# A gated cross-attention and quantised feed-forward kernel: first loads by halves, the last probabilities turned through a third bank, own result buffers for the last two tiles

## What is computed

```python
# attention, for each of 8 contexts; input1 = layernorm(x), input2 = ctx, both 256 x 512
theta_x = einsum('ld,bdt->btl', theta_w, input2) + theta_b        # latent 128
phi_x   = einsum('ld,bdt->blt', phi_w, input1) + phi_b
p       = softmax(einsum('btl,bls->bts', theta_x, phi_x))         # 512 x 512
g_x     = einsum('ld,bdt->btl', g_w, input1) + g_b
t_x     = einsum('bts,bsl->blt', p, g_x)
h       = relu((t_x - mean) * rsqrt(var + 1e-5) * ln_gamma + ln_beta)   # over 128 x 512
x       = x + tanh(g_xattn) * (einsum('ol,blt->bot', out_w, h) + out_b + input2)
# feed-forward; bitlinear(x, w) = quant8(rmsnorm(x)) @ ternary(w).T
x       = x + tanh(g_ffn) * bitlinear(silu(bitlinear(y, w1)) * bitlinear(y, w2), w3)   # y = layernorm(x)
```

## Time and profile before

| | |
|---|---|
| time, median of 3 runs | 303.57 us (303.13 to 303.72) |
| the profiled execution: its time | 304.05 us |
| its span, first to last instruction | 302.3 us |
| mean granted clock of TensorE | 0.999 of full speed |
| busy: TensorE, VectorE, ScalarE, GpSimd | 294.6, 240.7, 196.9, 194.1 us |
| attention, to the last context's last scores | about 119 us |
| passage | about 119 to 146 us |
| feed-forward, tiles 2 to 15 | about 146 to 302 us |

### The profile page before, as it was taken

How to read it: one execution, slowest core, us unless ns; L and a number is a source line. 1 busy time by engine, 2 the same in 40 slices (tenths; PEclk the granted TensorE clock), 3 DMA queues, 4 the chain that set the end, 5 groups by cost and what they waited for, 6 DMA issues and landing times.

```text
span 302.3 us, 4409 instructions
## 1 busy us (share of the span) xinstructions
PE 294.6 (97%) x1336; PEld 159.8 (53%) x1352; DVE 240.7 (80%) x541; ACT 196.9 (65%) x346; POOL 194.1 (64%) x294
## 2 busy tenths in 40 slices
PE   7899999999999999999999999999999999999995
PEld 5665757575757575544444444444444444444443
DVE  3799979796969796699988788887986896867862
ACT  1399898989989858787954736455455456355620
POOL 3360959594949187295988768576786786655710
PEclk9999999999999999999999999999999999999999
DMA  7999960496020001020325356144324351561354
GB/s 260 411 422 415 400 249 3 143 302 245 7 70 0 0 3 35 0 19 19 69 44 78 88 120 116 39 111 105 72 74 101 73 124 49 118 128 34 86 110 156
DMA packets 52792, 37.00 MB, mean 122 GB/s; under 512 B 43040, under 2 KB 43424, under 8 KB 51744
## 3 DMA queue, kind: packets, MB, share of 16 engines
q1 hardware_dynamic: 52480, 36.45, 42.4%
q10 hardware_dynamic: 288, 0.27, 0.3%
HBM read 22.02 MB, written 4.19 MB: 87 GB/s over the span
## 4 chain that ended last, share of the span: by engine, by line
PE 83%; DVE 6%; DMA 3%; issue 3%; SPq 2%; ACT 1%; POOLq 0%; DVEq 0%; POOL 0%
PE bank L1115 34%; PE bank L1133 14%; PE bank L1059 8%; PE bank L1039 7%; PE bank L1052 4%; PE bank L1074 4%; PE bank L1026 4%; PE bank L1018 3%; PE bank L1007 3%; DMA x<-x_dram 2%; DMA out_dram<-stage 1%; DVE stage L788 1%; SPq L266 1%; DVE x L726 0%; DVE xst L654 0%
## 5 line engine op out<-in xcount | busy, mean ns | idle before, releaser
L1115 PE MATMUL bank<-wq,stage 128*128 128x512 bf16 x499 | 112.4, 379 | 1.1 <-DVE x L726 0.4
L1115 PEld LDWEIGHTS bank<-wq,stage 128*128 128x128 bf16 x512 | 50.0, 98 | 62.4 <-issue 2.5
L788 DVE SCALAR_TENSOR_TENSOR stage<-bank,s,stage 128x512 f32<-128x512 f32 x64 | 47.5, 744 | 24.1 <-PE bank L1115 18.3
L543 ACT ACTIVATE xn<-stage 128x1024 f32<-128x1024 f32 x31 | 32.8, 1057 | 44.8 <-DVE stage L788 44.8
L535 ACT ACTIVATE stage<-bank,s 128x512 f32<-128x512 f32 x64 | 43.2, 681 | 17.0 <-PE bank L1115 14.8
L1133 PE MATMUL bank<-wq,prob 128*128 128x512 bf16 x221 | 50.3, 379 | 0.2
L409 POOL TENSOR_SCALAR stage<-stage,hsc 128x1024 f32<-128x1024 f32 x30 | 33.7, 1134 | 21.1 <-DVE hsc L819 21.1
L329 POOL TENSOR_SCALAR prob<-prob,rsum 128x512 f32<-128x512 f32 x30 | 20.2, 695 | 34.3 <-DVE rsum L690 34.3
L793 DVE TENSOR_REDUCE m<-stage 128x1 f32<-128x1024 f32 x31 | 37.7, 1215 | 0.8
L1039 PE MATMUL bank<-ph,th 128*128 128x512 f32 x96 | 36.0, 487 | 0.5 <-DVE ph L679 0.5
L1133 PEld LDWEIGHTS bank<-wq,prob 128*128 128x128 bf16 x224 | 21.9, 98 | 26.4
(11 more groups left out here) (113 smaller groups left out, 430.9 us busy)
## 6 DMA issues: line engine op xcount, KB each, us to landing
stage<-w1t_dram SPq DMA_DIRECT2D x4, 1024.0 KB, 12.0
stage<-w2t_dram SPq DMA_DIRECT2D x4, 1024.0 KB, 13.9
stage<-w3t_dram SPq DMA_DIRECT2D x4, 1024.0 KB, 6.5
out_dram<-stage SPq DMA_DIRECT2D x15, 256.0 KB, 2.3
x<-x_dram SPq DMA_DIRECT2D x7, 512.0 KB, 10.9
c_sb<-ctx_in_dram SPq DMA_DIRECT2D x7, 512.0 KB, 6.5
pc<-pack_c_dram SPq DMA_DIRECT2D x1, 640.0 KB, 16.0
x<-x_dram SPq DMA_DIRECT2D x2, 256.0 KB, 3.0
```

Source lines behind the costliest of these rows:

```text
L543: A.activation(junk, h_sb[t % 2][:, half * HF:(half + 1) * HF], ACT.Square, accum_out=ssq[:, half:half + 1]).then_inc(sq_done, 1)
L788: V.scalar_tensor_tensor(h_sb[k][:, c * 512:(c + 1) * 512], up_banks(n)[1][:, :], s12[:, u % 2, 1, k:k + 1], sil[n % 3], ALU.mult, ALU.mul ...
L1115: last = mm(bank[:, :], turned[:, row:row + P], wq[:, at:at + 512], start=q == 0, stop=q == KI - 1)
```

## The change

Loads: the halves of x 0 and context 0 go in turn, and `pack_b` goes as two DMAs, with a semaphore of its own for `g`'s weight. Eight warm-up matmuls stand where nine did. For context 0, GpSimd normalises three quarters and ScalarE the fourth, and `gated_context(0)` waits for `x_norm(0)`.

```diff
+        def result(t):
+
+            return c_sb[:, 1, t - (NT - 2)] if t >= NT - 2 else xo[t % 2]
...
+        def b_turn(i, c):
+
+            return banks[2] if (i, c) == (B - 1, 2) else banks[4] if i == B - 1 and c == 3 else b_pt[c % 2]
+
+        def turned_p(i, c):
+
+            return c_sb[:, 0, 0] if (i, c) == (B - 1, 2) else probT[:, 0] if i == B - 1 and c == 3 else probT[:, c % 2]
...
+        def b_total(k):
+
+            return banks[6] if k == 0 else b_st
...
             if n < 8:
-                return (pair0, pair0, pair2, pair0, pair2, pair1, pair0, pair2)[n]
-            return (pair0, pair2, pair1)[(n - 8) % 3]
...
+                return (pair0, pair2, pair0, pair2, pair0, pair1, pair2, pair0)[n]
+            return (pair2, pair0, pair1)[(n - 8) % 3]
...
             sp.dma_start(x2[:, 0:T], x_v[0][:, 0]).then_inc(xa_loaded, 16)
+            sp.dma_start(c_sb[:, 0, 0], c_v[0][:, 0]).then_inc(ca_loaded, 16)
             sp.dma_start(x2[:, T:2 * T], x_v[0][:, 1]).then_inc(x_loaded[0], 16)
-            sp.dma_start(c_sb[:, 0, 0], c_v[0][:, 0]).then_inc(ca_loaded, 16)
             sp.dma_start(c_sb[:, 0, 1], c_v[0][:, 1]).then_inc(c_loaded[0], 16)
-            sp.dma_start(pb[:, :], pack_b).then_inc(pb_loaded, 16)
+            sp.dma_start(pb[:, 0:D], pack_b[:, 0:D]).then_inc(pb_loaded, 16)
+            sp.dma_start(pb[:, D:2 * D], pack_b[:, D:2 * D]).then_inc(gw_loaded, 16)
...
+                if i == 0:
+                    pool.wait_ge(xn_ready, DH)
...
-                normalise(i - 1)
+                normalise(i - 1, TC - 1 if i == 1 else TC)
...
-                if 2 <= i <= 5:
+                if 3 <= i <= 5:
                     rounds((i - 2) // 2, 4 * (i % 2), 4 * (i % 2) + 2)
                 if i >= 2:
                     tx_root(i - 2)
-                if 2 <= i <= 5:
+                if i == 2:
+                    rounds(0, 0, 4)
+                elif 3 <= i <= 5:
                     rounds((i - 2) // 2, 4 * (i % 2) + 2, 4 * (i % 2) + 4)
...
             normalise(B - 1, 2)
+            rounds(2, 2, 3)
             tx_root(B - 2)
-            rounds(2, 2, 4)
+            rounds(2, 3, 4)
             prep_quant(1)
-            rounds(2, 4, 8)
+            rounds(2, 4, 6)
+            tx_root(B - 1)
+            rounds(2, 6, 8)
             root_h(0)
-            tx_root(B - 1)
             quant_h(0)
...
-                1: (None, (M, 0, 3), None, (M, 0, 4), None, (M, 0, 5), (M, 0, 6)),
-                2: ((M, 0, 7), (M, 1, 0), (M, 1, 1), (M, 1, 2), None, (M, 1, 3), (M, 1, 4)),
...
+                1: (None, None, None, (M, 0, 3), None, (M, 0, 4), (M, 0, 5)),
+                2: ((M, 0, 6), (M, 0, 7), None, (M, 1, 0), (M, 1, 1), (M, 1, 2), (M, 1, 3)),
...
                 act.wait_ge(pT_done, 4 * i + c + 1)
-                A.copy(probT[:, c % 2], b_pt[c % 2][:, :]).then_inc(pT_ready, 1)
+                A.copy(turned_p(i, c), b_turn(i, c)[:, :]).then_inc(pT_ready, 1)
...
+            def normalise(i):
+
+                act.wait_ge(rsum_ready, i + 1)
+                for c in range(2 if i else 3, TC):
+                    at = prob[:, i % 2, c]
+                    A.activation(at, at, ACT.Copy, scale=rsum[:, c:c + 1]).then_inc(pnorm_ready, 1)
...
-            act.wait_ge(rsum_ready, B)
-            for c in (2, 3):
-                A.activation(prob[:, 1, c], prob[:, 1, c], ACT.Copy, scale=rsum[:, c:c + 1]).then_inc(pnorm_ready, 1)
-            p_copy(B - 1, 0)
-            p_copy(B - 1, 1)
+            normalise(B - 1)
+            for c in range(TC):
+                p_copy(B - 1, c)
             silu(0, 0)
-            p_copy(B - 1, 2)
-            p_copy(B - 1, 3)
+            relu(B - 2)
             weight_sign(2, 0)
-            relu(B - 2)
+            silu(0, 1)
             weight_sign(2, 1)
-            silu(0, 1)
+            silu(0, 2)
             weight_sign(2, 2)
-            silu(0, 2)
...
             def down(t):
                 dve.wait_ge(dn_done, t + 1)
-                if t >= 2:
+                if 2 <= t < NT - 2:
                     dve.wait_ge(xo_free[t % 2], 16 * (t // 2))
-                V.scalar_tensor_tensor(xo[t % 2], b_down(t)[:, :], dq[:, t % 4:t % 4 + 1], x_tile(t), ALU.mult, ALU.add)\
+                V.scalar_tensor_tensor(result(t), b_down(t)[:, :], dq[:, t % 4:t % 4 + 1], x_tile(t), ALU.mult, ALU.add)\
                     .then_inc(xo_ready, 1)
...
+                if i == 0:
+                    low_part(i, ph, b_ph, 1, ph_ready, phl_ready)
                 if i + 1 < B:
                     x_stats(i + 1, 1)
                 else:
                     prep_scale(0)
-                if i == 2:
-                    weight_scale(0)
                 if i >= 3:
                     tx_dev(i - 2)
-                low_part(i, ph, b_ph, 1, ph_ready, phl_ready)
+                if i >= 1:
+                    low_part(i, ph, b_ph, 1, ph_ready, phl_ready)
                 if i == 2:
                     tx_dev(0)
...
+                if i == 2:
+                    weight_part(0)
+                row_max(i, 0)
                 if i == 0:
                     x_norm(1)
-                row_max(i, 0)
                 if i >= 2:
                     tx_var(i - 2)
                 if i >= 1:
                     residual(i)
                 row_max(i, 1)
+                if i == 2:
+                    weight_scale(0)
...
             tx_dev(B - 2)
             tx_gamma(B - 2)
             add_out(B - 3, 1)
-            hmul(0, 0)
             tx_var(B - 2)
             prep_max(1, 0)
             prep_max(1, 1)
             tx_norm(B - 2)
             prep_scale(1)
+            hmul(0, 0)
+            tx_mean(B - 1)
             row_stats(2, 0)
             row_stats(2, 1)
             prep_mean(2)
             hmul(0, 1)
-            tx_mean(B - 1)
+            add_out(B - 2, 0)
+            tx_dev(B - 1)
             hmul(0, 2)
-            absmax(0, 0)
-            add_out(B - 2, 0)
-            hmul(0, 3)
-            tx_dev(B - 1)
             add_out(B - 2, 1)
...
-            dve.wait_ge(xo_free[1], 16 * (NU - 1))
...
             def g(i):
-                if i >= 1:
+                if i == 0:
+                    pe.wait_ge(gw_loaded, 16)
+                else:
                     pe.wait_ge(exp_done, 4 * i)
...
-                if 4 * i + c >= 2:
-                    pe.wait_ge(pT_ready, 4 * i + c - 1)
+                if (i, c) == (B - 1, 2):
+                    pe.wait_ge(exp_done, 4 * B)
+                elif 4 * i + c >= 2:
+                    pe.wait_ge(pT_ready, 4 * i + c - 1 if (i, c) != (B - 1, 3) else 4 * i + 1)
                 if c == 1 and i >= 2:
                     pe.wait_ge(x2_ready, 2 * (i - 2) + 1)
                 for tc in range(TC):
-                    last = tr(b_pt[c % 2][:, tc * P:(tc + 1) * P], prob[:, i % 2, tc, c * P:(c + 1) * P], ident[:, :])
+                    last = tr(b_turn(i, c)[:, tc * P:(tc + 1) * P], prob[:, i % 2, tc, c * P:(c + 1) * P], ident[:, :])
...
-                last = mm(b_tx[:, :], gs[:, i % 2, c * P:(c + 1) * P], probT[:, c % 2], start=c == 0, stop=c == TC - 1)
+                last = mm(b_tx[:, :], gs[:, i % 2, c * P:(c + 1) * P], turned_p(i, c), start=c == 0, stop=c == TC - 1)
...
-                elif n == 2:
+                elif n == 1:
...
-                for part, bank in enumerate(b_last):
-                    for q in range(KF):
-                        if part == 0 and q % (KF // 2) == 0:
-                            pe.wait_ge(hT_loaded[1][q // (KF // 2)], 16 * NU)
-                        at = 2 * WCOLS + q * T + part * T // 2
-                        last = mm(bank[:, 0:T // 2], turned_h(NT - 1)[:, q * P:(q + 1) * P], wq[:, at:at + T // 2],
-                                  start=q == 0, stop=q == KF - 1)
-                    last.then_inc(dn_done, 1)
+                for half in range(2):
+                    pe.wait_ge(hT_loaded[1][half], 16 * NU)
+                    for part, bank in enumerate(b_last):
+                        for q in range(half * KF // 2, (half + 1) * KF // 2):
+                            at = 2 * WCOLS + q * T + part * T // 2
+                            last = mm(bank[:, 0:T // 2], turned_h(NT - 1)[:, q * P:(q + 1) * P], wq[:, at:at + T // 2],
+                                      start=q == 0, stop=q == KF - 1)
+                        if half == 1:
+                            last.then_inc(dn_done, 1)
...
-            for _ in range(9):
+            for _ in range(8):
...
-                if i == 2:
-                    weight_total(0, 2)
-                elif i >= 3:
+                if i >= 3:
                     mean_mm(i - 2, {4: 1, 7: 2}.get(i))
                 if i >= 3:
                     out_proj(i - 3, 1)
                 g(i)
                 if i == 2:
-                    mean_mm(0, 0)
+                    mean_mm(0)
                 if i >= 1:
...
                 scores(i, 1)
+                if i == 2:
```

(13 more changed lines are left out.)

50 lines of the change are left out of this document (26 added, 24 removed).

## The result

The changed kernel takes 300.75 us as the median of six runs (300.58 to 301.71), beside 303.58 for the kernel before in six runs (303.11 to 303.97). The ratio is 0.9913, with a 95% interval of 0.9897 to 0.9929: faster by 2.8 us.

The account below looks back on a forecast made before the run. TensorE, busy 294.6 of 302.3 us, was taken as the bound. Gains of 0.45 + 0.4 + 1.0 + 1.0 = 2.85 us took 304.05 to 301.2, or 300.7 against the median 303.57; range 300.0 to 301.3, 54%.

Parts of the forecast that it names:

- Start: Before the pipeline fills: reordered loads and VectorE work bring the second context's scores forward; 0.45 us gained, bounds -0.2 and 0.85.
- the start gives nothing: Rival at the start: x's second half comes late and the reciprocal at 17.03 doesn't move forward; 301.15 us, 10%.
- Third context: At `i` = 2, moving the weight total from before `g` to behind the second scores gains 0.4 us, between 0 and 0.56.
- Passage: From attention to feed-forward: earlier copies, `mean_mm` and `add_out` remove TensorE's waits; 1.4 us counted, 1.0 taken, bounds 0 and 1.4.
- thin covers: At the passage, `tx_dev` and the last sign would finish barely before TensorE wants them; so 1.0 of 1.4 us was taken.
- End: Last tiles: own result buffers remove the wait for store 13, one sum stays behind TensorE; 1.0 us gained, bounds -1.1 and 1.25.
- give its gain back: Rival at the passage: ScalarE or VectorE is late by 1 us and TensorE stands waiting; 301.7 us, 17%.
- lands late like store 13: Rival at the end: the last store itself lands 2.1 us late; 302.8 us, 10%.
- sign of being wrong: The forecast is wrong if TensorE waits at `var_mm(7)` or `down(0)`, or the last stores take over 3 us to land.
- slower by GpSimd's rounds stretching VectorE: Rival at the passage: VectorE's work stretches by 27%, `tx_dev` is 3.5 us late, a loss of 0.65; 304.2 us, 5%.

Follow-up runs that it names:

- e3_start: The changed kernel with the start undone (load order, `pack_b` in one load, low part of `ph`, nine warm-up matmuls, first normalising): 300.66 us.
- e4_passage: The changed kernel with the passage to the feed-forward undone (banks, buffers and the orders of all four engines there): 302.76 us.
- e9_cover: The changed kernel with `tx_dev(7)` one product later on VectorE, behind `hmul(0,2)` instead of ahead of it: 301.74 us.
- e7_result: The changed kernel with only the result buffers of the last two tiles undone, the new order of the last 32 matmuls kept: 302.08 us.
- e8_order: The changed kernel with only the order of the last 32 matmuls undone, the result buffers kept: 301.21 us.

## Why the prediction was right

The time said was 300.7 and 300.75 came out. That closeness is in part luck: the third context was put 0.3 too high and the passage 0.7 too low, the start's 0.45 has next to nothing behind it, and the two sides nearly cancel. What was right is where TensorE stood without work and that its waits at the passage and the end would go.

**Start, 0.45, measured 0.48 in the profiles.** The size came out, the reason only in part. The scores of the first context came 0.9 earlier, the reciprocal didn't move, and most of the gain was gone by the second context, all as worked out. But the step took the landings of x 1 in one profile (9.13) as given. 0.34 of the 0.48 is an earlier landing; what the order itself brings is 0 to 0.4 behind the landing, 0.2 is lost again outside the span, and e3_start, with all of it undone, is no slower. The rival "the start gives nothing" (10%) is closer to what the runs show.

**Third context, 0.4, measured 0.10.** This step failed. It asked who waits for the later total (GpSimd's rounds ran 38.00 to 43.2 and the normalising behind them began at 43.95, near the 43.6 of the forecast) and not what on TensorE comes next. `values(1,0)` needs two copies of ScalarE, whose queue was without a gap already in the profile before, from 26.14 on to the copy at 34.83, with four magnitude pieces ahead of the copy of `g`. Up to the second turn TensorE was 0.65 ahead (the idle 0.56, and `g`'s pass without a wait before it 0.09 shorter); 0.18 of that went to the total in its new place, about as priced, and 0.39 to `values(1,0)`, which starts 0.29 later behind its turn and takes 0.10 longer to the next scores, waiting for ScalarE's copy. That wait the prediction put at nothing. Taking one piece away gave exactly the 0.39 back.

**Passage, 1.0 taken of a counted 1.4, measured 1.73.** The term was mis-sized, and the measured value lies above the upper bound. The three places gave 0.38 for the moved `mean_mm` (0.3 counted), 0.49 for the copies (0.5) and 0.69 for `var_mm` and `add_out` (0.6). The remaining 0.17 stands at the last `out_proj`, ahead of `up(2,0)`: its four passes take 1.89 in the chain of before and of e4_passage and 1.72 in the changed kernel. What they waited for there wasn't traced. The prediction's first paragraph had the right figure: 25.0 us of work in 26.75. The stretch now runs 119.11 to 144.13, 25.0. The discount for thin covers was not needed: VectorE's `tx_dev(7)` came in time, with no reserve (e9_cover), and the last sign ended at 148.93, not near 151.3, since ScalarE's list had itself been waiting: behind the table load 3.3 us before (2.8 of them for VectorE's `hn`, 0.6 for TensorE), 0.6 after.

**End, 1.0, measured 1.07.** Right in size and mechanism. Undone alone, the buffers cost 1.26 and the order 0.23 in the profiles; they make more than 1.07 together because the order gives something only once the buffers have taken the landing out of the way.

**The rivals.** The passage didn't give its gain back. The two half stores at the end landed in 1.7 and 1.8 us, so "lands late like store 13" didn't come. The prediction's sign of being wrong, last stores over 3 us, did come for the two ahead of them (store 13 took 4.22, store 14 3.84), and nothing waits for those any more. Nor did "slower by GpSimd's rounds stretching VectorE": `tx_dev(7)` ended at 133.3, where 134.2 had been worked out. Elsewhere the stretch was real. In the third context the residual addition is at 0.68 again, as said, but the four rounds of weight 0 in one block, from 38.00 to 43.2, now stand beside the normalising of x 3. VectorE's timeline:

```profile
39.11 0.69 DVE L712 TENSOR_REDUCE nmax<-bank 128x1 f32<-128x512 f32 x1 [0.51 <-PE bank L1071]
39.72 2.52 DVE L697 TENSOR_SCALAR xn<-x,xmv,xrs 128x512 f32<-128x512 f32 x2
```

The two take 1.26 and 1.34 where all others in this profile take 0.54 to 0.55: 0.76 more each on average, close to the 0.8 that the prediction worked out by a rule of the Trainium skill (SBUF — State Buffer, "SBUF: two separate sides"), though it had in mind instructions with two inputs and these have one. That page of the Trainium skill names, beside those with two SBUF inputs, VectorE instructions in a 2-port performance mode. The lengths would fit that; no row shows in which mode these two ran. It costs nothing here, since with ScalarE's piece taken away the third context is 13.69 with the same stretch beside it.

## What to carry to other kernels

Where a wait of the busiest engine is removed, list what that engine needs next and from whom; here an engine whose queue ran without a gap ahead of that point took most of the gain, though it was 66% busy overall. Work of an engine in a stretch, set against the clock time that the stretch took, was a better bound than the sum of waits found one by one. A stage's gain is measured between two points inside each profile; between two profiles of the same kernel the landing of the first loads came 1.25 us apart and moved everything behind it by 1.0. And a span isn't the time: a change at the start can move what lies outside the span, here by 0.2 us.

## What the runs showed of the hardware

**A store lands late where an instruction load falls among the last stores.** In 13 of the 14 profiles of this case store 13 took 4.1 to 4.6 us to land (4.41 before, 4.60 in e7_result) and in e8_order 2.43; of the stores ahead of 285 us in the kernel before and the changed one, none took over 2.9. The transposes of the last tile ahead of it on the queue alone aren't the cause: they stand there in e8_order too, and store 12, between them and store 13, lands in 2.4 to 2.5 in all 14. What differs is one DMA packet of 16 KB that the profile counts as kind "instruction", on queue 8. It starts 1.3 to 2.5 us behind the issue of store 13 and takes 0.9 to 1.7 us in those 13 profiles; e8_order has none there. The DMA views of 293 to 297 us, first the changed kernel, then e8_order (busy share of the 16 DMA engines in tenths, 0.1 us each):

```profile
DMA  9999899999989998999730010100100001004999
...
q8 instruction: 1, 0.02, 2.0%
```

```profile
DMA  9999999999999999999930000000004999300000
```

From 295.1 to 296.6 the changed kernel's remaining packets go strictly one after another, as if all were left to the one DMA engine that had taken the instruction load; store 13 lands at 296.6. Over all 14 profiles, of 202 stores issued after 150 us with no such packet under way between issue and landing none took over 2.96 us; of the 36 with one, half took over 4.0 and up to 4.60. No experiment moved the packet, so the cause rests on that coincidence. If it is the cause, the buffers' gain hangs on it: where the packet is absent, as in e8_order, store 13 would be landed before TensorE ends. The Trainium skill (DMA: Bandwidth & Descriptors, "Queues, rings and completion order") says that a completion write lands after all earlier writes of the same DMA engine; that fits store 14, which lands 0.64 behind store 13 though issued 1.03 behind it, and no run here separates it from plain queueing.

**Landings of the first loads scatter.** The same kernel saw x 1 at 8.79 and at 10.04 us, and its two slowest runs of twelve, 301.71 and 301.88, stand 0.8 to 0.9 above their median; the second of them is the one with the late landing.

**One-column matmuls behind a wait cost more.** A pair takes 0.28 us in a full queue and 0.37 to 0.38 behind a wait, so a wait is worth a little more than its idle time.
